# First attention of a transformer kernel: score products in fp32 without split operands, one mask operation and one pair of root operations per pair of batch entries, low weight parts subtracted in pieces of 256 columns

## What is computed

```python
def _L0_xattn_ref(q, k, v, mask):        # q = layernorm(x), k = v = ctx, mask (16, 1, 128) of 0 and 1
    scores = einsum('bqd,bkd->bqk', q, k) * SCALE          # SCALE = 0.25
    scores = where(mask == 0, NEG, scores)                 # NEG = -1e10
    probs = softmax(scores, axis=-1) * (1.0 / (1.0 - DROPOUT_P))
    return einsum('bqk,bkd->bqd', probs, v)
x = x + _L0_xattn_ref(_layernorm(x), ctx, ctx, mask)
```

## Time and profile before

| quantity | value |
|---|---|
| median of 3 runs | 908.47 us |
| the profiled execution | 907.19 us |
| its span in the profile | 905.4 us |
| PE busy | 722.1 us (80%) |
| DVE busy | 687.6 us (76%) |
| POOL busy | 387.4 us (43%) |
| ACT busy | 344.3 us (38%) |
| first attention | about 0 to 130 us of the span |

### The profile page before, as it was taken

The page is one execution under the profiler, slowest core; times in us unless marked ns, Lnnn a source line. Parts: engine busy times, 40 slices in busy tenths (PEclk is TensorE's granted clock), DMA queues, the critical chain, the costliest instruction groups (busy, mean ns, idle before and its releaser), DMA issues.

```text
span 905.4 us, 30079 instructions
## 1 busy us (share of the span) xinstructions
PE 722.1 (80%) x10940; PEld 569.0 (63%) x10941; DVE 687.6 (76%) x1988; ACT 344.3 (38%) x686; POOL 387.4 (43%) x640
## 2 busy tenths in 40 slices
PE   2564642799999999999999999999888888843785
PEld 1343431577787787777787778887566555622563
DVE  4899966467777777777777777787999999874865
ACT  3333430343434444344344344453455445421210
POOL 2666643124344444353453444543344444425142
PEclk9976555799999999999999999999999999975698
DMA  7554420000000000000000000000222222112100
GB/s 283 193 167 168 156 104 1 3 2 3 2 0 0 0 0 0 0 0 0 0 0 0 0 0 2 2 15 25 65 92 78 74 81 81 53 43 94 25 1 6
DMA packets 22272, 41.18 MB, mean 45 GB/s; under 512 B 3340, under 2 KB 16278, under 8 KB 21832
## 3 DMA queue, kind: packets, MB, share of 16 engines
q1 hardware_dynamic: 21512, 38.70, 12.7%
q0 software_dynamic: 704, 1.71, 0.7%
HBM read 31.88 MB, written 8.91 MB: 45 GB/s over the span
## 4 chain that ended last, share of the span: by engine, by line
PE 65%; DVE 18%; issue 10%; POOL 3%; ACT 2%; DMA 2%; SPq 0%; DVEq 0%; POOLq 0%; ACTq 0%
PE ps L445 7%; PE ps L439 6%; PE ps L447 6%; PE ps L446 6%; PE ps L598 6%; PE ps L580 5%; DVE mx L1298 4%; PE ps L530 4%; PE ps L636 3%; PE ps L638 3%; PE ps L637 3%; PE ps L532 3%; PE ps L531 2%; PE ps L522 2%; PE ps L634 2%
## 5 line engine op out<-in xcount | busy, mean ns | idle before, releaser
L1707 POOL TENSOR_TENSOR rs<-mv,cst 128x1 f32<-128x1 f32 x164 | 35.0, 214 | 380.6 <-DVE mv L1095 343.5
L1298 DVE TENSOR_REDUCE mx<-ps 128x16 f32<-128x2048 f32 x48 | 109.8, 2287 | 1.6 <-PE ps L553 1.6
L950 ACT ACTIVATE pT<-ps 128x1024 f32<-128x1024 f32 x96 | 93.1, 1021 | 32.5 <-PE ps L580 30.4
L636 PE MATMUL ps<-xh,w_hi 128*128 128x128 bf16 x512 | 100.4, 220 | 0.0
L638 PE MATMUL ps<-xh,w_lo 128*128 128x128 bf16 x512 | 100.2, 219 | 0.0
L637 PE MATMUL ps<-xl,w_hi 128*128 128x128 bf16 x512 | 100.1, 219 | 0.0
L1709 POOL TENSOR_TENSOR rs<-rs,cst 128x1 f32<-128x1 f32 x164 | 92.2, 562 | 12.8
L445 PE MATMUL ps<-w_hi,hh 128*128 x256 | 70.1, 274 | 0.0
L446 PE MATMUL ps<-w_hi,hl 128*128 x256 | 69.8, 273 | 0.0
L447 PE MATMUL ps<-w_lo,hh 128*128 x256 | 69.8, 273 | 0.0
L530 PE MATMUL ps<-ycT_hi,w_hi 128*128 128x128 bf16 x256 | 59.6, 233 | 0.0
(11 more groups left out here) (353 smaller groups left out, 2534.9 us busy)
## 6 DMA issues: line engine op xcount, KB each, us to landing
stage<-in_w SPq DMA_DIRECT2D x16, 768.0 KB, 4.8
vec<-in_vec SPq DMA_DIRECT2D x4, 896.0 KB, 6.6
vec<-in_tw SPq DMA_DIRECT2D x12, 256.0 KB, 2.8
ctxc<-in_ctx SPq DMA_DIRECT2D x20, 128.0 KB, 2.1
comb<-x SPq DMA_DIRECT2D x16, 128.0 KB, 1.7
comb<-t SPq DMA_DIRECT2D x16, 128.0 KB, 1.8
shared<-x1b SPq DMA_DIRECT2D x16, 128.0 KB, 1.7
out<-x SPq DMA_DIRECT2D x16, 128.0 KB, 1.8
```

The costliest lines, as they stand in the source:

```text
L636: mm(dst, w(w_hi, c, j), xh[:, c, :], start=False, stop=False)
L950: A(pT[:, 8 * a:8 * a + 8, :].rearrange("p h q -> p (h q)"), ps[:, 2 * a:2 * a + 2, :].rearrange("p g k -> p (g k)"), ACT.Exp, scale=SCALE ...
L1298: nc.vector.tensor_reduce(mx[:, :], att.rearrange("p g s k -> p (g s) k"), AX.X, ALU.max, negate=True).then_inc(m_max, 1)
```

## The change

Five edits, all in the first attention.

- The transposed operands are copied by ACT in fp32 to one tile per entry (the memory of hh and hl, seen as fp32); DVE's low parts (L1144) are gone. PE multiplies them in fp32, two products per entry instead of six, and waits for ACT's copy (a_hi) instead of for a_split.
- The masks: one operation per pair, on 256 columns, gives the negative part. The 0 and 1 mask isn't stored; the masked scores are made by one scalar_tensor_tensor that compares the integer mask with 0 and multiplies by the scores in PSUM.
- Both roots of a pair in one addition and one power on 128 x 2, which wait for the second entry's variance.
- weights_low: six subtractions of 256 columns instead of one of 1536. The last one signals.
- Since a_split and a_m01 get no increments any more, two memsets at the start add 16 to each; the load of the second attention's weights waits for a_sm, since the masks are read until then.

```diff
+LOW = 256
-        yca_hi, yca_lo = (ycT_hi, hh), (ycT_lo, hl)
+        yca = tuple(t[:, :, :].rearrange("p c k -> p (c k)").bitcast(f32) for t in (hh, hl))
...
-            sp.wait_ge(a_neg, B)
+            sp.wait_ge(a_sm, B)
             sp.dma_start(wc_raw, wc_d).then_inc(wc_in, 16)
...
                 for j in range(2):
-                    pe.wait_ge(a_split, n[j])
-                    split_products(ps[:, 4 * j + 1, 0:128], lambda c: yca_hi[j][:, c, :], lambda c: yca_lo[j][:, c, :],
-                                   lambda c: yca_hi[j][:, KC + c, :], lambda c: yca_lo[j][:, KC + c, :],
-                                   KC).then_inc(a_s, 1)
+                    pe.wait_ge(a_hi, n[j])
+                    for c in range(KC):
+                        last = mm(ps[:, 4 * j + 1, 0:128], yca[j][:, 128 * c:128 * c + 128],
+                                  yca[j][:, D + 128 * c:D + 128 * c + 128], start=(c == 0), stop=(c == KC - 1))
+                    last.then_inc(a_s, 1)
...
-                    copy(yca_hi[j][:, 0:4, :], ps[:, 4 * j, :].rearrange("p (c k) -> p c k", k=128)).then_inc(a_hi, 1)
+                    copy(yca[j], ps[:, 4 * j, :]).then_inc(a_hi, 1)
...
+            nc.vector.memset(dsm[:, 7, 0:1], 0.0).then_inc(a_split, 16)
+            nc.vector.memset(dsm[:, 7, 1:2], 0.0).then_inc(a_m01, 16)
...
-                for j in range(2):
-                    m01, neg = h[:, 256 * j:256 * j + S], h[:, 256 * j + S:256 * j + 2 * S]
-                    mi = mask_i[:, ds(i * (2 * S) + j * S, S)]
-                    ts(m01, mi, 0.0, None, ALU.not_equal).then_inc(a_m01, 1)
-                    dve.wait_ge(a_m01, i * 2 + (j + 1))
-                    ts(neg, m01, 1.0, -NEG / SCALE_A, ALU.subtract, ALU.mult).then_inc(a_neg, 1)
+                ts(h[:, 0:2 * S], mask_i[:, ds(i * (2 * S), 2 * S)], 0.0, NEG / SCALE_A, ALU.is_equal,
+                   ALU.mult).then_inc(a_neg, 2)
...
-                for j in range(2):
-                    dve.wait_ge(a_hi, n[j])
-                    tt(yca_lo[j][:, 0:4, :], ps[:, 4 * j, :].rearrange("p (c k) -> p c k", k=128),
-                       yca_hi[j][:, 0:4, :], ALU.subtract).then_inc(a_split, 1)
...
-                    tt(tb2[j][:, 0:S], ps[:, 4 * j + 1, 0:S], h[:, 256 * j:256 * j + S], ALU.mult).then_inc(a_sm, 1)
+                    stt(tb2[j][:, 0:S], mask_i[:, ds(i * (2 * S) + j * S, S)], 0.0, ps[:, 4 * j + 1, 0:S], ALU.not_equal,
+                        ALU.mult).then_inc(a_sm, 1)
...
-                    tt(ta[j][:, 128:256], tb2[j][:, 0:S], h[:, 256 * j + S:256 * j + 2 * S], ALU.add).then_inc(a_sn, 1)
+                    tt(ta[j][:, 128:256], tb2[j][:, 0:S], h[:, S * j:S * j + S], ALU.add).then_inc(a_sn, 1)
...
+            def both(col):
+                return col.rearrange("p (a o) -> p a o", o=1).broadcast_to([128, 2, 1])
+
             def pair_roots(i):
-                for j in range(2):
-                    rstd(j, i * 2 + (j + 1), a_var, a_veps, a_rstd)
+                pool.wait_ge(a_var, i * 2 + 2)
+                tt(rs[:, 0:2, :], mv[:, 0:2, 1:2], both(cst[:, C_EPS:C_EPS + 1]), ALU.add).then_inc(a_veps, 2)
+                pool.wait_ge(a_veps, i * 2 + 2)
+                tt(rs[:, 0:2, :], rs[:, 0:2, :], both(halves), ALU.pow).then_inc(a_rstd, 2)
...
             def weights_low(i, j):
                 pool.wait_ge(w_hi_ready, i * 2 + (j + 1))
-                tt(w_lo[:, ds(i * (2 * WCH) + j * WCH, WCH)], stage[:, j, :], w_hi[:, ds(i * (2 * WCH) + j * WCH, WCH)],
-                   ALU.subtract).then_inc(w_lo_ready, 1)
+                for c in range(0, WCH, LOW):
+                    last = tt(w_lo[:, ds(i * (2 * WCH) + j * WCH + c, LOW)], stage[:, j, c:c + LOW],
+                              w_hi[:, ds(i * (2 * WCH) + j * WCH + c, LOW)], ALU.subtract)
+                last.then_inc(w_lo_ready, 1)
```

More of the change, by code:

```diff
@@ L1103, in _ @@
             nc.vector.memset(junk[:, 1:2], 0.0).then_inc(s_out, 16)
+            nc.vector.memset(dsm[:, 7, 0:1], 0.0).then_inc(a_split, 16)
+            nc.vector.memset(dsm[:, 7, 1:2], 0.0).then_inc(a_m01, 16)
             dve.wait_ge(s_shared, 16)
             dve.wait_ge(s_out, 16)
+            dve.wait_ge(a_split, 16)
+            dve.wait_ge(a_m01, 16)
             dve.wait_ge(x_in0, 16)
@@ L1711, in _ @@
             pool.wait_ge(cst_in, 16)
+            def both(col):
+                return col.rearrange("p (a o) -> p a o", o=1).broadcast_to([128, 2, 1])
             def pair_roots(i):
-                for j in range(2):
-                    rstd(j, i * 2 + (j + 1), a_var, a_veps, a_rstd)
+                pool.wait_ge(a_var, i * 2 + 2)
+                tt(rs[:, 0:2, :], mv[:, 0:2, 1:2], both(cst[:, C_EPS:C_EPS + 1]), ALU.add).then_inc(a_veps, 2)
+                pool.wait_ge(a_veps, i * 2 + 2)
+                tt(rs[:, 0:2, :], rs[:, 0:2, :], both(halves), ALU.pow).then_inc(a_rstd, 2)
             def gate_roots(i):
-                for j in range(2):
-                    rstd(2 + j, i * 2 + (j + 1), a_gvar, a_gveps, a_grstd)
+                pool.wait_ge(a_gvar, i * 2 + 2)
+                tt(rs[:, 2:4, :], mv[:, 2:4, 1:2], both(cst[:, C_EPS:C_EPS + 1]), ALU.add).then_inc(a_gveps, 2)
+                pool.wait_ge(a_gveps, i * 2 + 2)
+                tt(rs[:, 2:4, :], rs[:, 2:4, :], both(halves), ALU.pow).then_inc(a_grstd, 2)
             def weights_low(i, j):
                 pool.wait_ge(w_hi_ready, i * 2 + (j + 1))
-                tt(w_lo[:, ds(i * (2 * WCH) + j * WCH, WCH)], stage[:, j, :], w_hi[:, ds(i * (2 * WCH) + j * WCH, WCH)],
-                   ALU.subtract).then_inc(w_lo_ready, 1)
+                for c in range(0, WCH, LOW):
+                    last = tt(w_lo[:, ds(i * (2 * WCH) + j * WCH + c, LOW)], stage[:, j, c:c + LOW],
+                              w_hi[:, ds(i * (2 * WCH) + j * WCH + c, LOW)], ALU.subtract)
+                last.then_inc(w_lo_ready, 1)
             pair_roots(0)
```

## The result

The changed kernel takes 886.83 us (median of 4 runs, 884.72 to 889.57) against 908.35 for the kernel before (4 runs beside it, 907.76 to 911.54): a ratio of 0.974, 95% interval 0.971 to 0.977. The forecast was 888, with a range of 881 to 901. The profiled execution took 886.88 us, its span 885.1 instead of 905.4.

The account below looks back on a forecast made before the run. DVE stalls inside instructions until POOL's subtraction ends. Cycle 11.3 us instead of 14.30 gives 21.0 us by pair 7, net 20.2 after the dearer tail: 907.2 - 20.2 = 887.0, 888 on the median scale; range 881 to 901.

Parts of the forecast that it names:

- P: End of a pair's second subtraction on POOL; forecast at 38.8 us in pair 1, 49.8 in pair 2, 95.0 in pair 6.
- s = 0.65: Price in us of one 256-column piece of POOL's subtraction, start to start; expected between 0.61 and 0.76.
- One waiting instruction per piece: Beside POOL's pieces, one waiting DVE instruction passes per piece, so n of them take n pieces, at no visible POOL cost.
- rival (1): No gap between POOL's pieces, so DVE waits for all six: cycle 13.8 us, kernel about 908; chance 8%.
- (2): Dear pieces at L1723, handing over access costs POOL too: measurably slower from 1.0 us each, 920 at 1.1; chance 6%.
- (4): DVE passes POOL more freely than one instruction per piece: cycle 10.0 us or less, kernel 881; chance 8%.
- (3): Loads, scores and pow all at their dear ends, a piece near 0.7 us: kernel 900; chance 10%.
- P to H: From a pair's second subtraction's end on POOL to the next pair's bias end on DVE (L1160s): forecast 4.15 us.
- Pair 2: Third pair: POOL starts at 40.5 us after DVE's gate tokens, only additions wait; bias ends 42.6, second subtraction 49.8.
- Masks: One DVE operation of some 0.35 us per pair, issued about 0.3 before POOL's subtraction, so its stall should go.
- Scores: PE's fp32 score products for both entries take 2 to 4 us: covered at 2, just covered at 4.
- Loads: Every second pair, 896 KB of vectors go ahead of a weight buffer: up to 1.4 us on three pairs, 4 us.

Follow-up runs that it names:

- the last experiment: The changed kernel with masked scores as one addition from PSUM, pieces of 256, and vector loads moved behind the first attention's last weight load: 878.47 us.

## Why the prediction was right, and where it wasn't

**The time.** 887.0 us was forecast for the profiled execution, 886.88 was measured. That they agree to 0.1 us is luck: the sum missed the end of the phase by 1.4 us (129.85 - 20.2 = 109.65 against 111.02), and scatter in the rest of the span returned 1.5. Without that luck the time would still lie in the range of 881 to 901.

**Start.** The first cast of pair 1 was forecast for 28.35 and came at 28.84; 0.2 of this is the later landing of the masks. P of pair 1 was 39.23, forecast 38.8.

**Pieces, s = 0.65.** Right. Six take 3.80 to 4.08 us from the first start to the last end, forecast 3.95. Over the three sizes the straight line drawn from the earlier trace rows held to 0.02 us: 3.44/3 = 1.15 for 512 columns, 0.65 for 256, 0.41 for 128.

**One waiting instruction per piece.** Right, and this decides the case. It came from one place outside the changed stage; L1234 ended inside the next piece there. In the rows above a waiting instruction lasts 0.75 with pieces of 256 and 1.12 to 1.24 with pieces of 512, one piece each time; with 128 it lasts 0.50. The pieces do follow each other without a gap, as rival (1) had it (six of 0.685 us each take 3.85 to 4.0, so each starts before the last one's recorded end), and DVE passes all the same; that rival is refuted. So are (2), since a piece costs 0.65 and not 0.94 or more, and (4), since no steady pair took 10 us. Of (3) only the power was dearer than in the sum, by 0.09 us; the scores were cheaper, and the late loads mostly hidden.

**P to H.** Forecast 4.15; measured 4.14 in the pair shown, but 4.34 in the mean of the four steady pairs. That the cycle came out at 11.38, forecast 11.3, is in part two errors that cancel: P to H is 0.2 longer, the steps behind it 0.05 (3.18 for 3.23) and 0.1 (3.85 for 3.95) shorter. I had POOL's pieces start at P + 0.85, the tokens done at P + 2.25 and the additions at P + 3.55. With the power on two columns at 0.69 (forecast 0.6; one column 0.55) the pieces start at P + 0.94 at the earliest, tokens are done at P + 2.43 and additions at P + 3.78. In the pair shown POOL waited 0.38 us more for a cast, so the first token went ahead of the pieces, and the marks came at P + 2.22 and P + 3.57: the agreement of that pair with the forecast is luck too.

**Pair 2.** This step failed, by 0.9 us. I had POOL start at 40.5, when the cast would be done, "after DVE's gate tokens, so only the additions wait". The cast was over at 40.17, but the joined root only at 40.54 (forecast P + 0.85 = 39.65): P was 0.4 later, POOL waited 0.28 for the second statistics, and the power took longer. The tokens need this root and POOL's pieces stand behind it in POOL's order, so both started with it, and the tokens waited as in any other pair:

```profile
39.85 0.69 POOL L1725 TENSOR_TENSOR rs<-rs,cst 128x2 f32<-128x2 f32 x1
40.51 4.00 POOL L1730 TENSOR_TENSOR w_lo<-stage,w_hi 128x256 f32 x6
...
40.69 0.63 DVE L1100 TENSOR_SCALAR x<-x,mv,rs 128x256 f32 x1 [1.33 <-POOL rs L1725]
41.24 0.75 DVE L1100 TENSOR_SCALAR x1b<-x,mv,rs 128x256 f32 x1
```

H was 43.66 + 0.26 = 43.92 (forecast 42.6), P of pair 2 50.95 (49.8). From P of pair 1 to H it was 4.7 us instead of 3.8; the other 0.4 had come from pair 1. With this and 0.08 us more in each of four cycles (11.38 against 11.3), P of pair 6 came at 96.46 (95.0). The tail from H of pair 7 (100.49) took 10.53 us, forecast 10.45.

**Masks.** The mechanism was right: the one operation is begun 0.1 us ahead of the subtraction (forecast 0.3) and lasts 0.28. But in the first two pairs POOL starts its second subtraction before the mask, and there the mask waits too (0.76 at 21.74 and at 36.69). What the prediction didn't say is whose gain the 5.3 us of stall are. The sum took them away once, which is right for the whole change. As a reading of the edits it would mislead: the pieces alone give 16.3, the masks alone 9.0, the scores alone 1.8, which would add up to 27.1, and together it is 18.8. The stall of the mask operation, 2.8 us inside DVE and 1.5 on the path at the root, is gone with either edit.

**Scores.** Covered, as forecast, and cheaper. The products of both entries take 1.2 us in the pair shown (71.87 to 73.08, at a granted clock of 1.00 in that stretch); I had priced 2 to 4 from a row at the low clock. The only places where DVE waits for them are in pair 0, 2.82 and 0.50 us at 14.87 and 15.66. On the path the edit is worth 0.3 us, not the 1.2 of work that it removes.

**Loads.** Forecast up to 1.4 us on three pairs as a risk. They were late in steady pairs (ACT idle for 1.27 us before 73.58), but mostly hidden by the round through DVE: of the 1.27 POOL saw 0.38. They show once the additions are out of the way, as the last experiment has it. The wait of SP for the last mask cost nothing visible.

**The advice on tile size.** I had set the Trainium skill (VectorE: DVE Perf Modes, the TRN2 errata: tiles of at least 512 elements) against pieces of 256. That section speaks of VectorE and ScalarE instructions, and the pieces are POOL's, so it was no evidence here. A fixed part exists on POOL too, 0.19 us. Still 512 columns ended the phase 5.5 us later than 256, counted from its start: the waits of the other engine outweigh it. 128 columns ended it 4.2 us later, and there the fixed part is what counts.

## What to carry to other kernels

An instruction that lasts many times longer beside another engine's long one was waiting here, not working: compare the longest and the shortest of its group, and find what runs beside it. Cutting the long instruction up gives the others one passage per piece, and it pays as long as the waits that are saved on the path exceed the fixed part of each piece; both sides can be read from rows before anything is built, and of the three sizes tried the middle one was best. Two edits that remove one wait are not two gains: price each also with the other already made, and once a stall is gone, look at the loads that it had hidden. And where a difference is as small as the scatter of the load that a phase starts with, count from that load.

## What the runs showed of the hardware

- DVE's tensor_scalar on 255 columns, input and output in SBUF, lasted 2.92 us beside POOL's subtraction of 3.09, as the one on 256 columns does (3.06). I had expected it to pass, on the reading that only an even number of columns brings in the second access. The Trainium skill (VectorE: DVE Perf Modes, Mode 2×_2P — use both read ports for one tensor) also admits a count that is odd and equal on both sides to the mode that uses the second access; by that rule the trace agrees, and my expectation came from reading only half of it. It also means that this run didn't take the second access away, so it is no test of whether that access is the cause.
- On POOL a power on 128 x 2 takes 0.69 us and one on 128 x 1 0.55; the addition takes 0.19 on either. Two roots in turn took 1.58 us to the next subtraction, joined they take 0.98 (85.02 to 86.00): 0.6 us of POOL's time. A root for one entry is done 0.82 us behind the start of its addition, the joined one 1.03.
- A passage of DVE costs POOL little. The subtraction that three or four DVE instructions pass takes 3.99 us for its six pieces (75.23), the one that meets only the mask 3.85 (70.02), and one that meets nothing 3.80 (30.51): some 0.05 us for each.
